# Eight zero columns ahead of one product in each out and down projection

## What is computed

```
...
        xz = x @ w_in                                   # 256 -> 2 x 512
        xp, z = jnp.split(xz, 2, axis=-1)
        xc = silu(depthwise_conv(xp, conv_w) + conv_b)  # 4 taps, causal
        def step(h, xt):
            h = h * 0.9 + 0.1 * (xt @ w_B)              # state of 16
            return (h, h @ w_C)
        y = ys.transpose(1, 0, 2) * silu(z)
        return y @ w_out                                # 512 -> 256, "out projection"
...
        # per sequence: the two best of eight experts, chosen by its first token
        h = jax.nn.gelu(einsum(x, W1g) + b1g)           # 256 -> 256 per expert
        o = einsum(h, W2g) + b2g                        # 2 x 256 -> 256, "down projection"
        return jnp.sum(o, axis=1) / k
    x = x + attn(layernorm(x))
    x = x + ffn(layernorm(x))
```

## Time and profile before

| | us |
|---|---|
| median of 3 runs | 510.57 (510.38 to 511.04) |
| the profiled execution's own time | 510.43 |
| its span | 508.5 |
| TensorE busy | 503.3 (99%) |
| TensorE's weight loads busy | 447.5 (88%) |
| VectorE busy | 453.2 (89%) |
| ScalarE busy | 401.0 (79%) |
| GpSimd busy | 343.1 (67%) |

### The profile page before, as it was taken

How to read it: one execution, slowest core, us unless ns; L and a number is a source line. 1 busy time by engine, 2 the same in 40 slices (tenths; PEclk the granted TensorE clock), 3 DMA queues, 4 the chain that set the end, 5 groups by cost and what they waited for, 6 DMA issues and landing times.

```text
span 508.5 us, 9829 instructions
## 1 busy us (share of the span) xinstructions
PE 503.3 (99%) x3026; PEld 447.5 (88%) x3026; DVE 453.2 (89%) x900; ACT 401.0 (79%) x694; POOL 343.1 (67%) x384
## 2 busy tenths in 40 slices
PE   8999999999999999999999999999999999999997
PEld 8878799889898989989899998989989899898997
DVE  6999999999998899979999899998999889896773
ACT  4886958888869789697886969879797888969454
POOL 4866587649694696928969197772977649773291
PEclk9999999999999999999999999999999999999999
DMA  8940104435151542606235171542604333130102
GB/s 263 291 177 1 42 1 167 124 125 167 62 175 56 156 132 83 206 0 206 83 124 165 41 217 30 165 124 78 211 31 147 111 124 126 50 116 0 43 2 83
DMA packets 53378, 57.27 MB, mean 113 GB/s; under 512 B 8682, under 2 KB 49642, under 8 KB 53226
## 3 DMA queue, kind: packets, MB, share of 16 engines
q1 hardware_dynamic: 51498, 56.67, 34.8%
q10 hardware_dynamic: 1856, 0.31, 0.3%
HBM read 35.46 MB, written 21.50 MB: 112 GB/s over the span
## 4 chain that ended last, share of the span: by engine, by line
PE 93%; DVE 1%; POOL 0%; issue 0%; DVEq 0%
PE blk L1257 15%; PE blk L1258 15%; PE blk L1262 15%; PE tok L1374 12%; PE tok L1376 12%; PE tok L1375 12%; PE turn L1415 3%; PE turn L1418 3%; PE blk L1437 3%; PE turn L1209 1%; POOL normed L408 0%; PE tok L1262 0%; PE tok L1257 0%; PE tok L1258 0%; PE turn L1258 0%; PE turn L1257 0%
## 5 line engine op out<-in xcount | busy, mean ns | idle before, releaser
L958 DVE SCALAR_TENSOR_TENSOR conv<-blk,tap_w,conv 128x512 f32<-128x512 f32 x192 | 130.1, 742 | 7.8 <-ACT conv L651 7.1
L462 POOL TENSOR_TENSOR y_lo<-gate,y_hi 128x512 fp32r<-128x512 f32 x57 | 72.2, 1297 | 36.6 <-ACT y_hi L580 36.6
L1257 PE MATMUL blk<-xn_hi,w_in_hi 128*128 128x512 f32 x228 | 89.5, 393 | 0.0
L1258 PE MATMUL blk<-xn_hi,w_in_lo 128*128 128x512 f32 x228 | 89.0, 391 | 0.0
L427 POOL TENSOR_TENSOR xc_lo<-conv,xc_hi 128x512 fp32r<-128x512 f32 x59 | 70.9, 1218 | 8.8 <-ACT xc_hi L580 8.0
L1374 PE MATMUL tok<-w_out_hi,y_hi 128*128 128x256 f32 x256 | 72.1, 282 | 0.0
L1376 PE MATMUL tok<-w_out_hi,y_lo 128*128 128x256 f32 x256 | 71.8, 281 | 0.0
L1375 PE MATMUL tok<-w_out_lo,y_hi 128*128 128x256 f32 x256 | 71.8, 281 | 0.0
L1262 PE MATMUL blk<-xn_lo,w_in_hi 128*128 128x512 f32 x228 | 70.3, 389 | 0.0
L1374 PE MATMUL tok<-w_hi,hid_hi 128*128 128x256 f32 x248 | 69.9, 282 | 0.0
L1376 PE MATMUL tok<-w_hi,hid_lo 128*128 128x256 f32 x248 | 69.6, 281 | 0.0
(11 more groups left out here) (185 smaller groups left out, 1320.9 us busy)
## 6 DMA issues: line engine op xcount, KB each, us to landing
spill<-normed SPq DMA_DIRECT2D x25, 512.0 KB, 2.8
normed<-spill SPq DMA_DIRECT2D x100, 128.0 KB, 2.9
out<-x_mid SPq DMA_DIRECT2D x30, 256.0 KB, 2.8
x_mid<-in_L_attn_x SPq DMA_DIRECT2D x29, 256.0 KB, 2.8
x_in<-in_L_attn_x SPq DMA_DIRECT2D x14, 512.0 KB, 4.6
w_all<-in_L_ffn_W SPq DMA_DIRECT2D x2, 2048.0 KB, 11.6
b_all<-in_L_ffn_b SPq DMA_DIRECT2D x1, 1024.0 KB, 13.1
gate<-in_L_attn_w_in SPq DMA_DIRECT2D x2, 256.0 KB, 4.7
```

Source lines behind the costliest of these rows:

```text
L462: nc.gpsimd.tensor_tensor(y_lo[:, j, :], gate_of(o, j), y_hi[:, j, :].bitcast(F32), ALU.subtract).then_inc(y_lo_set, 1)
L958: nc.vector.scalar_tensor_tensor(cols, blk[j][:], tap_w[:, j, t:t + 1], cols, ALU.mult, ALU.add).then_inc(tap_added, 1)
L1257: mm(dst, whi(k), his(k), start=(k == 0), stop=False)
L1258: mm(dst, wlo(k), his(k), start=False, stop=False)
```

## The change

w_out_hi and w2_hi become views of wider buffers that have 128 further columns in front (ROOM). The last eight of these columns are set to zero once, by two GpSimd copies from a small buffer of zeros, in GpSimd's opening ahead of w_out_lo. In `tokens`, for h = 0, j = 0 and the second tile (n = 1), the high x high product streams 264 columns instead of 256, the eight zero columns first, and its output begins eight columns earlier in the bank, in the first tile's last eight columns, to which it adds zero. Each out_proj call waits in addition for the zeros. The output of the kernel stays what it was.

```diff
+ROOM, ZEROS = 128, 8
...
-        w_out_hi, w_out_lo = sb("w_out_hi", [P, JD, D], F32R), sb("w_out_lo", [P, JD, D], F32R)
-        w2_hi, w2_lo = sb("w2_hi", [P, TOP_K, KD * D], F32R), sb("w2_lo", [P, TOP_K, KD * D], F32R)
+        w_out_wide = sb("w_out_wide", [P, ROOM + JD * D], F32R)
+        w_out_hi, w_out_lo = w_out_wide[:, ROOM:].rearrange("p (j d) -> p j d", j=JD), sb("w_out_lo", [P, JD, D], F32R)
+        w2_wide = sb("w2_wide", [P, ROOM + TOP_K * KD * D], F32R)
+        w2_hi, w2_lo = w2_wide[:, ROOM:].rearrange("p (t c) -> p t c", t=TOP_K), sb("w2_lo", [P, TOP_K, KD * D], F32R)
+        no_columns = sb("no_columns", [P, ZEROS])
...
             nc.gpsimd.memset(decay[:], DECAY).then_inc(consts_set, 1)
+            nc.gpsimd.memset(no_columns[:], 0.0).then_inc(consts_set, 1)
...
                 norm1(2)
+                pool.wait_ge(consts_set, 5)
+                nc.gpsimd.tensor_copy(w_out_wide[:, ROOM - ZEROS:ROOM], no_columns[:]).then_inc(zeros_set, 1)
+                nc.gpsimd.tensor_copy(w2_wide[:, ROOM - ZEROS:ROOM], no_columns[:]).then_inc(zeros_set, 1)
                 pool.wait_ge(w_hi_set, 6 + REP)
                 weights_lo(w_out_lo[:], raw_out, w_out_hi[:])
...
-            def tokens(h, j, last, his, los, whi, wlo):
+            def tokens(h, j, last, his, los, whi, wlo, wide=None):
...
                     dst = tok[h][:, n * D:(n + 1) * D]
-                    mm(dst, his[:, j, rows], whi, start=(j == 0 and n == 0), stop=False, skip_group_check=True)
+                    if wide is not None and n == 1:
+                        mm(tok[h][:, D - ZEROS:2 * D], his[:, j, rows], wide[:, ROOM - ZEROS:ROOM + D], start=False, stop=False,
+                           skip_group_check=True)
+                    else:
+                        mm(dst, his[:, j, rows], whi, start=(j == 0 and n == 0), stop=False, skip_group_check=True)
...
-                    ins = tokens(h, j, j == JF - 1, hid_hi, hid_lo, w2_hi[:, t, cols], w2_lo[:, t, cols])
+                    ins = tokens(h, j, j == JF - 1, hid_hi, hid_lo, w2_hi[:, t, cols], w2_lo[:, t, cols],
+                                 w2_wide if h == 0 and j == 0 else None)
...
             def out_proj(o, h):
+                pe.wait_ge(zeros_set, 2)
                 pe.wait_ge(done, o * 2 + h + 1)
...
-                    ins = tokens(h, j, j == JD - 1, y_hi, y_lo, w_out_hi[:, j, :], w_out_lo[:, j, :])
+                    ins = tokens(h, j, j == JD - 1, y_hi, y_lo, w_out_hi[:, j, :], w_out_lo[:, j, :],
+                                 w_out_wide if h == 0 and j == 0 else None)
```

More of the change, by code:

```diff
@@ L152, in build_block @@
         mixed = sem("mixed")
+        zeros_set = sem("zeros_set")
         mid_set = sem("mid_set")
```

## The result

| | median, us | lowest to highest | ratio to before, 95% interval |
|---|---|---|---|
| before, timed beside it | 510.48 | 509.97 to 511.04, 4 runs | |
| changed | 517.34 | 517.32 to 517.45, 4 runs | 1.0135 [1.0123, 1.0147] |

The changed kernel is 6.9 us slower. The forecast was 505.9, in a range of 505.0 to 511.0, and the slowest of its cases, 513.2, is 4 us short of what was measured. The page of the changed kernel, where the earlier trace rows stood before: the span is 515.5 us, TensorE has the clock of 1.0 throughout, and the chain still lies on it.

A forecast was written before the change was run, and what follows sets the result against it. TensorE's product-to-product distances were taken as the bound. Short pace in the projections gave 4.4 us plus 0.25 us carried past state_out, 4.65 less than 510.57: 505.9 us, range 505.0 to 511.0.

The forecast's parts named there:

- What bounds the kernel: Whole kernel: TensorE, busy 99% of the span, sets the time through distances between product starts; other engines matter only if late.
- the two paces: 256-column out and down products start 0.1177 us apart (long, reading 281 ns) or 0.1134 us (short, 276 ns).
- Eight columns more: Out and down projections: 32 products of 264 columns cost 3.4 ns more each, 0.11 us in all.
- the overlap: Wide product adding zeros to columns the preceding product wrote: a wait of at most 0.4 us in all, taken as 0.
- the added wait: Wait for the zeros before every out_proj, 32 times: 1.6 us without the queue's lead, taken as 0.
- GpSimd: GpSimd's opening: a memset and two copies of 8 columns, nothing to 1.5 us for both copies, hidden.
- the slower case: Out and down projections slow through the opening's pace, 513.2 us, or a dearer overlap or wait; chance 0.12.
- the opening's pace: Third pace, seen in the opening's 256-column products: reading 283 ns, about 2 ns longer than the long pace.
- The products of 512 columns stay at 0.226: Expected sign in the changed trace: start distances of 512-column products, in us, remain unchanged.
- The pace: Out and down projections: the wide product's slip brings the short pace, 4.65 us less; chance 0.56 for both projections.
- (d): Trace reading: not every disturbance changes pace; after the transposes at 74.7 the projection goes on at 281.
- VectorE's room: VectorE has 2.3 us of room per 30.5 us stretch, against 0.35 us shrinkage, so TensorE's gain passes whole.

The follow-up runs named there:

- e4: Changed kernel with the zeros' buffer behind all other buffers and every product 256 columns wide: 510.38 us, ratio 0.9994 to the kernel before.
- e1: Changed kernel with the zeros' buffer placed behind all other buffers, the 32 wide products kept: 506.79 us, ratio 0.9930 to the kernel before.
- e2: Kernel before with only an unused 32-byte buffer added ahead of w_in_hi: 518.08 us, ratio 1.0148.
- e3: Changed kernel with buffers, zeros, waits and addresses kept but every product 256 columns wide: 517.96 us, ratio 1.0146 to the kernel before.
- e13: Kernel before with 32 bytes ahead of xn1_hi, moving streamed operands and weights together by 32 bytes: 510.34 us, ratio 0.9995.
- e14: Kernel before with streamed operands alone at offset 32 within 128 bytes, weights at their old offsets: 521.17 us, ratio 1.0218.

## Why the prediction was wrong

*What bounds the kernel, and the two paces*: held. TensorE is busy 99% of the span in all sixteen traces, and 281 and 276 ns were the right marks at the old offsets. (The 61.10 us of the earlier trace rows are one turn of two steps, not two turns; the room of 2.3 us for each step stands.)

*Eight columns more, the overlap, the added wait*: held. e4 prices waits, copies and rooms at nothing (510.38 against 510.56), and e1 shows no stall at the overlap: the wide product's distance is 121 ns.

*GpSimd*: this is the step that failed. I priced the buffer of zeros by its memset and its copies, which are hidden as I said, and not by its 32 bytes. I had read the buffers' declarations as text of no cost and listed no rival in which an operand's address changes, so the slower case (513.2, the opening's pace) had another mechanism and was 4 us short. e2 measures the missing term: 7.5 us, most of it in products that the diff does not mention. It stood in the text as "The products of 512 columns stay at 0.226"; they went to 0.233, and that is 6.9 us of the changed kernel's loss.

*The pace*: the guess that a slip changes it was right, and the size was 1.05 us too large even at the old offsets, where the wide products gave 3.6 us (e4 to e1) for a forecast of 4.65. The out projections gave their 2.5 (2.8 in the trace); the down projections gave 1.3 of the 2.1 counted for them. In chunks 1 and 2 they ended in the long pace, and the short pace is not carried over state_out in the loop: 0.25 us had been counted for that. One reading behind it was wrong. Under (d) I took the 281 after the transposes at 74.7 for a pace that a disturbance had left alone, and found no place where the short pace turned into the long one. But just ahead of those transposes the down projection was in the short pace (four products of L1376 from 72.7 to 73.8; the first stands right behind a wait):

```profile
L1376 PE MATMUL tok<-w_hi,hid_lo x4: 276/280/286, 72.7 to 73.8; 128*128 128x256 f32 x4
```

The starts from 72.87 to 73.78 are 0.1138 apart. So the trace of before already had a change from short to long, and the slip could be expected to work both ways, as it did in e1. At the changed kernel's offsets the pair of 113.4 and 117.7 ns is not there: the distances go in patterns from 115 to 122 ns, with means of 117.5 and 118.6, and the wide products were worth the 0.6 us that part the changed kernel from e3.

*VectorE's room*: held; e1 has one wait of TensorE more than before, 0.5 us behind VectorE in the opening, and none in the loop.

What stays open: why an unequal offset costs 6 to 7 ns on 512 columns, whether it is to be counted modulo 128 bytes or more, what the paces are inside the engine, and whether it is the wide product's columns or its start address that makes the slip, the same with four columns as with eight. The Trainium skill (TensorE: Matmul & The Clock Gate, section Step-by-step: what each phase is for) says that TensorE reads streamed operand and weights through two ports of their own, and that loading the next weights takes no read bandwidth from the product that runs. The trace agrees with this only up to some 3% of a 512-column product: the mean distance is 227.5 ns in e13 and 234.2 in e14, where the offset of the two against each other is another. Whether that is bandwidth at the ports, no run here shows.

## What to carry to other kernels

Where TensorE is the bound and every product loads new weights, an inserted or resized buffer can change every product whose operands lie behind it: compare the operands' offsets before and after, and keep new small buffers behind everything that TensorE reads (e1, e4), or in sizes of 512 bytes a partition, as the rooms were. Smaller multiples of 128 are not tried here. Judge a change at the operands' old addresses before judging its idea; here the idea was worth -0.7% and its buffer +1.5%. If one kind of product shows two durations in the trace, look at what stood in front of it: one product of another form can choose between them, in either direction.

## What was not expected of the hardware

512-column products start 227.5 to 227.9 ns apart where weights and streamed operand lie at the same offset, and 233.2 to 234.2 ns apart where the weights lie 32, 64 or 96 bytes past it. 256-column products with new weights each had mean distances from 115.7 to 120.0 ns over these layouts, with the same shapes; at the old layout a distance of 113.4 or 117.7 is held for tens of products, and one product with four or eight columns more, which also starts 16 or 32 bytes earlier, moved them from 117.7 to 113.4; with eight it moved them back too.
